# Swapping which heads GpSimd and VectorE multiply in the per-token attention of a transformer layer

## The reference

```python
q = (x @ wq.T).reshape(b, s, H, HD)          # H = 16, HD = 128
k = (x @ wk.T).reshape(b, s, H, HD)
v = (x @ wv.T).reshape(b, s, H, HD)
q = apply_rope(q, inv_freq); k = apply_rope(k, inv_freq)
scores = jnp.einsum('bshd,bstd->bsht', q, k) / jnp.sqrt(jnp.float32(HD))
weights = jax.nn.softmax(scores, axis=-1)
attn = jnp.einsum('bsht,bstd->bshd', weights, v)
attn = attn.reshape(b, s, HIDDEN) @ wo.T
x = x + attn                                 # x above was _layernorm(x)
x = x + ffn(_layernorm(x))                   # 2048 -> 8192 -> 2048, silu(g)*u
```

## Time and profile before

| | us |
|---|---|
| time, median of 3 runs | 8143.17 |
| lowest and highest of the 3 runs | 8050.18, 8248.4 |
| the profiled execution, its own time | 7855.62 |
| span of its slowest core (core 2) | 7854.0 |
| spans of the 8 cores | 7821.6 to 7854.0 |

### The profile page before, as it was taken

One profiled execution on the slowest core, in us unless ns is written; L12 is line 12 of the kernel. 1 busy time (PEld: TensorE's weight loads), 2 busy tenths in 40 slices (PEclk: granted clock), 3 DMA queues, 4 the chain that ended last, 5 costly groups with the idle time before them and its releaser, 6 DMA issues.

```text
span 7854.0 us, 47030 instructions; the slowest of 8 cores (7821.6 to 7854.0 us)
## 1 busy us (share of the span) xinstructions
PE 3977.2 (51%) x17070; PEld 1769.9 (23%) x17408; DVE 1978.2 (25%) x1216; ACT 1202.3 (15%) x1450; POOL 1876.0 (24%) x443
## 2 busy tenths in 40 slices
PE   0475757001111111111111598769966898679965
PEld 0232323000000000000000243224422343234422
DVE  2100000365666666665664000000000000000000
ACT  3321222001111111111111211001100111001100
POOL 0000000385566666665564000000000000000000
PEclk9987878555555555555555799779987999889987
DMA  6224242301111111111121565456644765466644
GB/s 150 87 83 101 81 104 80 78 25 58 51 62 58 46 45 46 46 46 58 51 66 38 149 153 129 91 135 154 152 90 91 175 152 115 91 154 153 139 86 112
DMA packets 1769861, 741.46 MB, mean 94 GB/s; under 512 B 1632336, under 2 KB 1689712, under 8 KB 1759392
## 3 DMA queue, kind: packets, MB, share of 16 engines
q1 hardware_dynamic: 1658048, 520.16, 29.0%
q10 hardware_dynamic: 99840, 167.80, 5.9%
q0 software_dynamic: 11744, 50.46, 3.1%
HBM read 604.10 MB, written 167.77 MB: 98 GB/s over the span
## 4 chain that ended last, share of the span: by engine, by line
PE 43%; DMA 20%; DVE 15%; POOL 9%; issue 8%; ACT 4%; ACTq 1%; SPq 0%; DVEq 0%; POOLq 0%
PE ps_dn L99 13%; PE ps_g L99 11%; PE ps_u L99 11%; POOL prod L90 9%; DVE prod L90 6%; DMA wdb<-wd_sc 6%; PE ps_p L99 6%; DVE sc_sb L90 4%; DVE red L90 3%; DMA wg_sc<-cvout 3%; DMA wd_sc<-cvout 2%; PE ps_y L99 2%; DMA wu_sc<-cvout 2%; DMA cvin<-gwT 2%; DMA wo_bf<-woT 1%
## 5 line engine op out<-in xcount | busy, mean ns | idle before, releaser
L99 PE MATMUL ps_y<-wo_bf,aTs 128*128 128x512 bf16 x995 | 288.8, 456 | 2161.6 <-ACT yrow_t L90 1876.9
L99 PE MATMUL ps_dn<-h_sb,wdb 128*128 128x512 bf16 x4013 | 1050.2, 426 | 485.5 <-DMA wdb<-wd_sc 473.0
L90 POOL TENSOR_TENSOR prod<-pbf,vt 128x2048 bf16<-128x2048 bf16 x176 | 1080.8, 6175 | 266.6 <-DVE red L90 266.6
L99 PE MATMUL ps_g<-xn2q,wgb 128*128 128x512 bf16 x4016 | 926.8, 381 | 128.6 <-DMA wgb<-wg_sc 124.6
L99 PE MATMUL ps_p<-wst,xnT 128*128 128x512 bf16 x3010 | 761.0, 416 | 348.7 <-ACT prow L90 230.4
L99 PE MATMUL ps_u<-xn2q,wub 128*128 128x512 bf16 x4012 | 919.4, 379 | 4.4
L90 POOL TENSOR_TENSOR prod<-qt,kt 128x2048 bf16<-128x2048 bf16 x176 | 748.6, 4291 | 647.1 <-DVE sc_sb L90 647.1
L118 POOL DMA_DIRECT2D out_rows<-outt x16 | 8.6, 538 | 3599.8 <-DVE outt L90 3507.1
L99 PEld LDWEIGHTS ps_dn<-h_sb,wdb 128*128 128x128 bf16 x4096 | 434.6, 107 | 1101.1 <-issue 727.8
L90 DVE TENSOR_REDUCE red<-prod 128x128 f32<-128x2048 bf16 x256 | 580.8, 2284 | 363.4 <-POOL prod L90 354.8
L90 DVE TENSOR_REDUCE sc_sb<-prod 128x16 f32<-128x2048 bf16 x256 | 579.7, 2284 | 266.7 <-POOL prod L90 258.4
(11 more groups left out here) (52 smaller groups left out, 871.1 us busy)
## 6 DMA issues: line engine op xcount, KB each, us to landing
wgb<-wg_sc SPq DMA_DIRECT2D x256, 512.0 KB, 5.6
wub<-wu_sc SPq DMA_DIRECT2D x256, 512.0 KB, 5.5
wdb<-wd_sc SPq DMA_DIRECT2D x128, 1024.0 KB, 6.9
wg_sc<-cvout ACTq DMA_DIRECT2D x128, 256.0 KB, 2.0
wu_sc<-cvout ACTq DMA_DIRECT2D x128, 256.0 KB, 2.1
wd_sc<-cvout ACTq DMA_DIRECT2D x128, 256.0 KB, 2.4
cvin<-gwT SPq DMA_DIRECT2D x128, 128.0 KB, 3.8
xrow<-x_own SPq DMA_DIRECT2D x8, 2048.0 KB, 11.1
```

The lines of the kernel that those rows point to most:

```text
L90: ins = getattr(self.h, opname)(*args, **kw)
L99: ins = self.h.matmul(*args, **kw)
```

## The change

In both head loops GpSimd's 11 heads are now the first eleven, 0 to 10, and VectorE's five are the last, 11 to 15. Before, VectorE had 0 to 4 and GpSimd 5 to 15. The counts, the buffers, the reduces and all waits by name stay.

```diff
@@ -494,7 +494,7 @@
                 for hh in range(H):
                     pb = hh % NPROD
-                    peng = "vector" if hh < H - POOL_SC else "gpsimd"
+                    peng = "gpsimd" if hh < POOL_SC else "vector"
                     qbc = bc_ap(qt[bi], hh * 128, [[0, 16], [1, 128]])
@@ -536,7 +536,7 @@
                 for hh in range(H):
                     pb = hh % NPROD
-                    peng = "vector" if hh < H - POOL_AT else "gpsimd"
+                    peng = "gpsimd" if hh < POOL_AT else "vector"
                     pbc = bc_ap(pbf, hh * 16, [[0, 128], [1, 16]])
```

## The result

| | before | changed |
|---|---|---|
| median of all runs, us | 8050.2 (26 runs) | 8051.5 (26 runs) |
| lowest run, us | 7860.3 | 7948.0 |
| profiled execution, slowest core, us | 7854.0 | 7947.2 |

Ratio of changed to before 1.0096, 95% interval [1.0057, 1.0134]: about 1% slower, within the 2% called no change. Executions come in two kinds: of 25 further ones of the kernel before, six, with a granted TensorE clock near 0.76 on both dies, took 7851 to 7893 us, and nineteen, with a die at 0.70 to 0.74, took 7987 to 8375; the ratio leaves the second kind out and the medians of all runs contain them, which is why the medians agree while the ratio and the profiles do not. Forecast were +96 us on the profiled time (ratio 1.012); the profiles differ by 93 us. The forecast of 8239 us, and its range from 8130 to 8370, missed all the same: the changed kernel's median is 8051.5.

The account below looks back on a forecast made before the run. Phase CD's GpSimd and VectorE queues bound the change: scores -70.8, attention +166.6, together +96 us, giving 7951 on the profiled 7855.6 and 8239 on the three runs' median 8143.2; range 8130 to 8370.

Parts of the forecast that it names:

- The bound and the part of the kernel touched: Phase CD, about 2850 of 7854 us: its changes move the span one for one; the feed-forward stays untouched.
- Score loop, 50.5 us: Steady tile's score loop: 50.5 us in place of 56.6, a gain of 6.1 us.
- the tail: Cast, six conversions, projection and norm after a tile's attention loop: unchanged at 37.1 us, VectorE idle for 27.8.
- The head start: GpSimd runs four score products of the next tile early, in the tail, where VectorE idles 27.8 us.
- rival 1: Score products start only when VectorE enters the loop; score and attention loops each 7.6 us worse, +253 us, 8396; chance 0.07.
- Attention loop, 92.6 us: Steady tile's attention loop: 92.6 us in place of 82.0, a loss of 10.6 us.
- the turns: VectorE's last attention products and GpSimd's early score products exclude each other, VectorE going next: 3.0 us per tile.
- The edges: Tile 0's scores lose 17.6 us, tile 1's gain only 3.0, the last tile's attention loses 7.6.
- The sum: Over all tiles: scores -70.8 us, attention +166.6 us, together +96 us, 1.2% slower.
- (2): GpSimd wins the turns at VectorE's last attention products, 8.7 us more per tile: +226 us, 8369; chance 0.06.
- (3): VectorE's last pairs slide into gaps between reduces in both loops, some 700 us faster, 7440; chance 0.05.
- 8194: Forecast time if the two kinds of product don't exclude each other at all: +51 us.

Follow-up runs that it names:

- e4: The whole change, with GpSimd's first score product of each tile also waiting for VectorE's last instruction before the score loop; ratio 1.0309 against before.
- e2: The kernel before, with the new head order in the attention loop only; ratio 1.0170, +121.7 us over the phase.
- e3: The whole change, with GpSimd's first score product also waiting for attention reduce 15 of the tile before; ratio 1.0113, phase +55.4 us against before.
- e5: The kernel before with the same counts, VectorE's heads spread to 2, 5, 8, 11 and 14 in both loops; ratio 0.9897.
- e9: The whole change on a kernel with projection, norm and six conversions moved out of the tail; no ratio, phase -270.3 us against before.
- e8: The kernel before with projection, norm and six conversions moved out of the tail, and heads alternating between engines; ratio 0.9123, median 7191.6 us.
- e6: The kernel before with heads alternating in both loops, eight even on GpSimd, eight odd on VectorE; ratio 0.9703.

## Why the prediction was right and where it was wrong

**The bound and the part of the kernel touched.** Right. Outside the phase the profiled spans differ by 2 us: 7854.0 - 2743.2 = 5110.8 and 7947.2 - 2834.6 = 5112.6; the eight cores have 5079 to 5111 and 5082 to 5113. (The page shows GpSimd busy in slices 8 to 22, not 8 to 21 as read; no number hangs on it.)

**Score loop, 50.5 us.** Measured 50.5. From cast to exponential the 14 steady tiles gain 87.8 us in sum, for 85.4 forecast; the rest, 0.2 us a tile, is the tail. The forecast's 37.1 us for it came from a tile longer than most. So tiles are 180.8 us apart, not 182.3, but before they are 176.6 on average, not 177.8: +4.2 for +4.5 forecast. The head start is there in each, and e4 shows that without it the loop loses as much as rival 1 said.

**Attention loop, 92.6 us.** Measured 94.6 - 84.1 = 10.5 over before's 82.0, that is 92.5. The part of it that I took from other pairs of instructions, the turns between a VectorE attention product and a GpSimd score product, was 3.0 us: the last tile, which has no next scores, is 3.0 us shorter (91.6), and e2 and e3, without such neighbours, have 91.6 in all tiles.

**The edges.** First tile: from GpSimd's first product to the exponential 65.5 against 47.9, 17.6 us. Second tile: 53.6 against 56.5, 2.9 of 3.0.

**The sum.** +96 forecast, +91.4 over the phase, +93.2 in the span.

**Rivals.** The head start was not lost (1). GpSimd did not win the turns (2): two of five VectorE products were held up by 1.5 us, none by 3.9. No pair slid past a waiting reduce (3): VectorE's gaps of 2.95 us are still there.

**What failed is the last step of the sum:** "I carry the same 96 us over: 8239 us". The three runs' median, 8143.2, was no property of the kernel: 26 runs of the same program have 8050.2. The profiled execution, 7855.6, was a fourth time of the same kernel, and it lies just below the lowest of the 26, 7860.3. No record shows the cores of those three runs, but 7855.6 lies in the lower of the two bands given under the result and 8143.2 in the upper, which is wide. That gap of 288 us belonged into the range. I added 96 us to the higher of the two and let the range start 64 us below 8194, so that neither the better known 7951 nor anything near it was inside.

The better median would not have saved the step: 8050.2 + 96 = 8146, and the changed kernel's median is 8051.5. Such a median depends on how many runs fall near the lowest. Within 22 us of it lie 12 of the changed kernel's 26 runs and 3 of before's, so the medians differ by 1 us while the lowest runs differ by 88 and the profiles by 93. Whether the edit has a part in that count, or it is chance, no run shows. In its chances (0.83 for within 2%) the text did not depend on this; in its time it did, wholly.

## What to carry to other kernels

Two engines that exclude each other in some instructions could be forecast here by walking both queues in order with measured durations: the change came out within 5 us of the measured phase, though e5's first tile was 10 us off and e9 was 26, where products collided otherwise than walked. The mean durations of a table hide this, since they contain the waits. Work put first on one engine gains only what it can do while the other is idle for another reason, and it costs the other engine's products moved behind the last wait: look for that idle time first, and ask whether it can be removed instead, which here was worth some 5% alone and 9% with the heads spread. When the few times shown of a kernel scatter by more than the change, forecast the difference against the profiled execution and let the range of the time reach from there.

## What the runs showed of the hardware

- Even a VectorE instruction with two inputs of one element per partition waited for GpSimd's multiply: st_msq took 4.78 us in e8 and e9 beside GpSimd, 0.16 us in the changed kernel without. VectorE's reduces of prod never waited: 2.27 to 2.29 us in all kernels. The Trainium skill ("SBUF — State Buffer", section "Who interferes with whom") says both, the lock for two SBUF inputs and none for a tensor_reduce; the traces agree.
- Who goes next when both wait is not settled. The same section of the Trainium skill says that issue order decides. In e5's attention loops VectorE's product (in one tile issued at 1742.76, beside a GpSimd product that ended at 1745.69) went ahead of GpSimd's next, whose buffer had been free for over 5 us (79 of 80 products took 6.4 us, a wait of 2.8); in the first score loop of e5, e6 and e8 one VectorE product each took 6.8 us, a wait of 5.6, which is the rest of GpSimd's current product and all of its next. The runs don't show what sets the two cases apart, and nothing was tried on it.
